# First aggregation pass of a graph network: the mask tile moves to PSUM, and the window sums share four banks

## What is computed

```python
msg = feat[src]
h_sum = jax.ops.segment_sum(msg, dst, num_segments=n)
deg = jax.ops.segment_sum(jnp.ones((src.shape[0],), dtype=feat.dtype), dst, num_segments=n)
h_neigh = jnp.where(deg[:, None] > 0, h_sum / jnp.maximum(deg, 1.0)[:, None], 0.0)
return h_neigh @ W_neigh.T + b_neigh
```

## Time and profile before

| quantity | value |
|---|---|
| median of three runs | 9503.14 us (9498.97 to 9505.79) |
| the profiled execution's own time | 9495.59 us |
| its span in the profile | 9493.7 us |
| first pass, first gather to last add | 33.6 to 1147.5 us |
| busy share over the span: PE, DVE, POOL | 69%, 52%, 73% |

### The profile page before, as it was taken

The page is one execution under the profiler, slowest core; times in us unless marked ns, Lnnn a source line. Parts: engine busy times, 40 slices in busy tenths (PEclk is TensorE's granted clock), DMA queues, the critical chain, the costliest instruction groups (busy, mean ns, idle before and its releaser), DMA issues. The chain is left out here.

```text
span 9493.7 us, 138066 instructions
## 1 busy us (share of the span) xinstructions
PE 6504.4 (69%) x30150; PEld 4954.7 (52%) x30150; DVE 4890.2 (52%) x16263; ACT 1137.3 (12%) x2527; POOL 6905.4 (73%) x7491
## 2 busy tenths in 40 slices
PE   6777656666777788835888866665566668866665
PEld 5656534444666654525777634443455557744443
DVE  7766644333555543685777644444322226744445
ACT  0000000000000003730000000000222227610000
POOL 6777777777777777777777777777677776547775
PEclk6666655555766678558999955555777878965555
DMA  3111112222333332005777621112677765422221
GB/s 86 49 48 50 41 44 53 53 53 53 111 105 105 105 103 74 2 11 153 221 223 222 192 66 53 53 53 58 141 192 193 193 175 149 151 103 53 53 53 53
DMA packets 665600, 935.71 MB, mean 99 GB/s; under 512 B 276165, under 2 KB 444542, under 8 KB 664958
## 3 DMA queue, kind: packets, MB, share of 16 engines
q0 software_dynamic: 271792, 607.35, 24.0%
q1 hardware_dynamic: 294130, 322.66, 10.9%
q10 hardware_dynamic: 99548, 4.42, 0.9%
HBM read 790.86 MB, written 143.03 MB: 98 GB/s over the span
## 5 line engine op out<-in xcount | busy, mean ns | idle before, releaser
L555 PE MATMUL sage_window<-sage_hot,sage_message 128*128 128x128 f32 x4992 | 1443.4, 428 | 683.4 <-DMA sage_message<-t_x,all_src 312.7
L555 PE MATMUL block_window<-block_hot,block_message 128*128 128x128 f32 x3328 | 1184.0, 456 | 714.3 <-DMA block_message<-t_rel,all_src 327.9
L555 PEld LDWEIGHTS sage_window<-sage_hot,sage_message 128*128 128x128 f32 x4992 | 1070.4, 291 | 1056.5 <-issue 719.4
L555 PEld LDWEIGHTS block_window<-block_hot,block_message 128*128 128x128 f32 x3328 | 792.7, 296 | 1081.4 <-issue 623.4
L374 POOL DMA_INDIRECT block_message<-t_rel,all_src x832 | 785.2, 944 | 423.8 <-issue 253.3
L477 DVE TENSOR_TENSOR first_acc<-first_acc,sage_window 128x128 f32 (+1 forms) x1664 | 591.5, 355 | 962.4 <-PE sage_window L555 957.7
L374 POOL DMA_INDIRECT block_message<-in_x,all_src x832 | 849.8, 1021 | 287.8 <-issue 252.9
L1946 POOL DMA_INDIRECT eh_message<-t_q,all_position x880 | 831.3, 945 | 278.2 <-issue 267.4
L374 POOL DMA_INDIRECT gat_message<-t_h,all_src x832 | 791.2, 951 | 262.8 <-issue 252.8
L374 POOL DMA_INDIRECT rgcn_message<-t_rel,all_src x832 | 785.9, 945 | 262.5 <-issue 253.3
L374 POOL DMA_INDIRECT sage_message<-t_x,all_src x832 | 785.7, 944 | 262.2 <-issue 253.2
(11 more groups left out here) (419 smaller groups left out, 10279.0 us busy)
## 6 DMA issues: line engine op xcount, KB each, us to landing
eh_window<-t_p SPq DMA_DIRECT2D x880, 64.0 KB
t_hidden<-eh_hidden SPq DMA_DIRECT2D x110, 512.0 KB, 3.0
sc_rows<-t_hidden SPq DMA_DIRECT2D x110, 512.0 KB, 3.5
eh_low_rows<-t_low SPq DMA_DIRECT2D x110, 256.0 KB
t_rel<-n_h SPq DMA_DIRECT2D x49, 512.0 KB, 2.6
eh_message<-t_q,all_position POOLq DMA_INDIRECT x880
block_message<-in_x,all_src POOLq DMA_INDIRECT x832, 2.5
sage_message<-t_x,all_src POOLq DMA_INDIRECT x832, 2.5
```

The source lines that it names most:

```text
L555: last = nc.tensor.matmul(ps[k][:, b, :], message[u][:, f:f + P], hot[:, u, j * P:(j + 1) * P], start=(j == 0), stop=(j == heads - 1))
```

## The change

In the first pass alone (`places_edges`), the eight windows lie two to a bank in four banks, and `inside` lies in PSUM (two banks' worth, 1024 floats of which 832 are used) where it lay in SBUF. Because two windows share a bank, DVE waits for the second of the two before it adds the first, so that it never reads a bank that PE is writing. In iteration 13 PE waits for `find_starts` before it writes the seventh window of the second half, which shares the bank of `ps_own`; before, it waited ahead of the eighth. The other passes keep their eight windows in eight banks, and their DVE waits are unchanged.

```diff
-        ps = [pb(f"window{k}", [P, outs, P]) for k in range(HU)]
+        if places_edges:
+            banks = [pb(f"windows{k}", [P, 2, outs, P]) for k in range(HU // 2)]
+            ps = [banks[k // 2][:, k % 2] for k in range(HU)]
+            inside = pb("inside", [P, 1024])[:, 0:T]
+        else:
+            ps = [pb(f"window{k}", [P, outs, P])[:] for k in range(HU)]
...
-        inside = sb("inside", [P, T]) if places_edges else None
...
-                    if k == HU - 1:
+                    last_of_bank = u | 1 if places_edges else u
+                    if last_of_bank % HU == HU - 1:
                         dve.wait_ge(e.half_used[h], half0 + it + 1)
                     else:
-                        dve.wait_ge(e.window_ready, done0 + it * (U - 2) + u + 1 - h)
+                        dve.wait_ge(e.window_ready, done0 + it * (U - 2) + last_of_bank + 1 - h)
...
-                    if starts and u == U - 1:
+                    if starts and u == U - 2:
                         pe.wait_ge(starts_used, 1)
```

More of the change, by code:

```diff
@@ L389, in count_block @@
                 dve.wait_ge(counted, j)
-                nc.vector.tensor_scalar(inside[:], m.src_high[:, 0:T], m.iota[:, bass.ds(j, 1)], 0.0, ALU.is_equal, ALU.add,
+                nc.vector.tensor_scalar(inside, m.src_high[:, 0:T], m.iota[:, bass.ds(j, 1)], 0.0, ALU.is_equal, ALU.add,
                                         accum_out=m.in_block[:, bass.ds(j, 1)]).then_inc(counted, 1)
@@ L394, in mask_block @@
                 dve.wait_ge(placed, j + 1)
-                nc.vector.tensor_scalar(inside[:], m.src_high[:, 0:T], m.iota[:, bass.ds(j, 1)], None, ALU.is_equal).then_inc(masked, 1)
+                nc.vector.tensor_scalar(inside, m.src_high[:, 0:T], m.iota[:, bass.ds(j, 1)], None, ALU.is_equal).then_inc(masked, 1)
             def rank_block(j):
                 dve.wait_ge(masked, j + 1)
-                nc.vector.tensor_tensor_scan(rank[:], m.ones[:, 0:1].to_broadcast([P, T]), inside[:], m.block_start[:, bass.ds(j, 1)],
+                nc.vector.tensor_tensor_scan(rank[:], m.ones[:, 0:1].to_broadcast([P, T]), inside, m.block_start[:, bass.ds(j, 1)],
                                              ALU.mult, ALU.add).then_inc(ranked, 1)
@@ L415, in place_block @@
             def place_block():
-                nc.vector.copy_predicated(position[:], inside[:].bitcast(I32), rank[:]).then_inc(placed, 1)
+                nc.vector.copy_predicated(position[:], inside.bitcast(I32), rank[:]).then_inc(placed, 1)
             def own_hots(it):
@@ L427, in own_add @@
                 nodes = m.acc[:, 0:outs, bass.ds(it * P, P)]
-                nc.vector.tensor_tensor(nodes, nodes, ps_own[:], ALU.add).then_inc(own_used, 1)
+                nc.vector.tensor_tensor(nodes, nodes, ps_own, ALU.add).then_inc(own_used, 1)
             def fuse_add(it):
@@ L476, in turn @@
                         dve.wait_ge(own_used, it + 1)
-                    nc.vector.tensor_tensor(window, window, ps[k][:], ALU.add).then_inc(e.window_used, 1)
+                    nc.vector.tensor_tensor(window, window, ps[k], ALU.add).then_inc(e.window_used, 1)
                     if nodes_too and own and u == 2:
```

## The result

The changed kernel takes 9440.4 us, the median of four runs, against 9502.3 us for the kernel before: a ratio of 0.9935, 95% interval 0.9923 to 0.9948, or 61.9 us less. Timed once more, with other kernels beside it, it took 9442.9 us against 9505.0 (0.9936, 0.9921 to 0.9951). The forecast was 9447, with a range of 9438 to 9480.

The account below looks back on a forecast made before the run. POOL's chain of gathers was taken to bound the first pass, PE and DVE following with room left. 63.1 - 6.3 - 0.6 - 0.3 = 55.9 us off the profiled 9495.6 gave a median of 9447 us, range 9438 to 9480.

Parts of the forecast that it names:

- The relief, 63.1 us: Placing stages: running sum and predicated copy no longer hold POOL's gathers, taking 63.1 us off its chain.
- The mask's 0.42 us: DVE's mask, written to PSUM, takes its slow form of 1073 ns, adding 0.42 us per block.
- The sum and the copy at no cost: DVE's running sum and predicated copy, reading the mask from PSUM, take no longer: 0 added.
- The hand-over, 2.43 us: Last add to next half's first add: waiting for two windows raises it from 1.57 to 2.43 us.
- 10.7: Time in us that PE and DVE need for a half that places a block, data always there.
- POOL's wait of 6.3 us: Stage with two blocks per iteration: lateness of DVE beyond what buffers store makes POOL wait 6.3 us.
- 16.3: DVE's lateness in us over the stage with two blocks: 22 halves x 0.74.
- the 10 us that I had for what the buffers store: POOL's buffers let it run ahead, so 10 us of lateness is only stored and made up in later iterations.
- A: Rival: PE and DVE become the bound in both placing stages; 28 us gained, 9475 us; chance 0.19.
- B: Rival: the running sum still holds POOL, gathers stay at 1111 and 1025 ns; 9503 us or slightly more; chance 0.11.
- C: Rival: the running sum takes twice its time reading PSUM; 26 us slower, 9529 us; chance 0.06.
- My point of decision for C, 12.06 us: Length of a placing half from which C decides, 1.35 us above the forecast's 10.7.

Follow-up runs that it names:

- the four kernels: Windows in pairs and mask in SBUF, against the kernel before, with nothing, ranks, ones, or both in PSUM: 9498.7, 9489.5, 9453.9, 9443.5 us.
- pairs_only: The kernel before with only the windows put in pairs, the mask staying in SBUF (the pairs alone): 9498.7 us, ratio 0.9999.
- slow_mask_sbuf: Windows in pairs, ones and ranks in PSUM, mask in SBUF made by the slower form that also sums its output: 9444.2 us, 0.9938 of the kernel before.
- the extra half sum: The changed kernel with a second running sum over half the mask after each block's own: 9470.9 us, 0.9961 of the kernel before.
- the extra sum: The changed kernel with a second running sum over the whole mask after each block's own: 9490.2 us, 0.9986 of the kernel before.

## Why the prediction was right, and where its sum was off

**The relief, 63.1 us: right.** The busy time of the 832 gathers fell by 849.8 - 787.6 = 62.2 us. The last add came 60.3 us earlier: 0.9 us went to idle time ahead of the gathers, and 1.0 to a longer stretch between the last gather and the last add, for which I had 0.6. The reasoning from the adds (one operand in SBUF and one in PSUM, beside gathers of 946 ns) is what the four kernels showed for each operand in turn. The split: against the pairs alone, 45 us from the running sum, 9 from the copy, and, from the traces, some 6 from the mask. In the timelines of the kernel before, the excess of gathers that began inside the three operations was 50, 9 and 1 us (3 for the mask, with those that it held from their middle); the shares of sum and mask depend on how the operations fall against the gathers, which the pairs moved (43, 18 and 6 us in the kernel with the pairs alone). In one thing it was luck: I had counted the mask's slow form only as a cost. With the windows in pairs the fast form held gathers for 6.9 us (`pairs_only`), against 3.2 in the kernel before, and the slow form spared that too.

The rule of the Trainium skill (SBUF — State Buffer, "Who interferes with whom") is borne out in all three clauses: two SBUF inputs hold POOL, one does not, and of the two forms of the mask only the faster one does; the form that also writes its accumulator is the one that the page leaves out of the two-port modes. My prediction left out a condition of the page: for two SBUF inputs it speaks only of a GpSimd instruction that reads SBUF. The gather does, as it takes its row numbers from an SBUF tile.

**The mask's 0.42 us: right** (0.43, from the medians of 648 and 1080 ns). **The sum and the copy at no cost: right**, 1940 and 1071 ns against 1945 and 1078. The Trainium skill's surcharge for PSUM (Perfetto Trace Analysis, "Optimizing Scalar/DVE Operations") did not show where PSUM was read. Where it was written the count's main part grew by 7 ns, 1073 to 1080.

**The hand-over, 2.43 us: the upper end of what came.** In the changed kernel the median in the stage with two blocks was 2.4 us and the mean 2.2, with the shortest 1.6. In 13 of the 22 halves the granted clock was at the lower level all through the hand-over, which took 2.44 us in the mean; in the other 9 it was at the upper level for a part, and they took 1.86. DVE's own work from the first add to the end of the last was 8.0 to 8.8 us, 8.2 in the mean, against the 8.28 of my sum. So a half took 10.38 us (228.3 / 22) and not 10.7. (In that sum I called 409.60 the end of an add. It is the start of the next operation, and the add ends at 409.67; the sum, which goes from start to start, is not touched.)

**POOL's wait of 6.3 us: the term that failed.** It did not wait in a placing stage, in either trace of the changed kernel. 22 halves at 0.38 us over POOL's 10.0 make 8.4 us of lateness, not 16.3, and that fits into the 10 us that I had for what the buffers store. The 10 us are borne out by `slow_mask_sbuf`: its stage with two blocks took 230.8 us, 10.8 over POOL's 220, and near its end POOL began to wait, five times, by 0.2 to 0.5 us each beyond the usual 0.30. The changed kernel's timeline shows the lateness stored and worked off: from the start of a gather to its add it was 6.0 us at the first iteration of that stage, 14.7 us when it ended, and 4.9 us four iterations later. Of the 0.3 us by which a half was shorter than my sum, 0.23 lie in the hand-over above: I took the clock's lower level for every half, from one stretch of 0.50. Without the term the sum is 55.9 + 6.3 = 62.2 us, against 61.9 measured.

**The rivals.** A (28 us gained, PE and DVE the bound in both stages) did not come, but the extra half sum shows its edge: 1.0 us more on DVE per block, and 0.2 more of hand-over, cost 28 us, nearly all of it in the stage with two blocks (255.2 against 228.3 us). B is excluded by the gathers, C by the 1940 ns. My point of decision for C, 12.06 us a half with a block, left out that the halves without one would be shorter: with the extra sum, at 12.5 us a half in the stage with two (274.3 / 22), the kernel was still 15 us faster than before.

## What to carry to other kernels

Where POOL issues indirect DMAs back to back and sets the pace, look at the spread of its instruction's duration, not at its waits: gathers of 1.9 and 2.6 us among ones of 0.94 were DVE's doing, and no wait row told of it. There, a DVE operation with two SBUF inputs is worth giving one input in PSUM, even a constant one. A form of an operation that is faster by itself can hold the gathers where the slower one does not: 7.0 us over the pass for the mask of 0.65 us, nothing for the one of 1.07. A stage whose follower is slightly too slow is free as long as the buffers store its lateness and a later stage works it off, so sum lateness over the stage and compare it with the store before counting it.

## What was not expected

The pairs alone raised PE's clock in the counting stage, in which nothing else had changed. From 60 to 300 us, in the kernel with the pairs alone (busy of PE, PEld, DVE, ACT, POOL, then granted clock):

```profile
60.00:300.00 240.00, 167.14 (x796) 143.04 (x795) 172.84 (x499) 0.00 (x0) 180.16 (x191) 0.73 0.20 52
```

The kernel before has 0.64 there and PE busy for 188 us with as many matmuls; the changed kernel has 0.75. The pairs make PE wait longer at each half: from last add to first add it was 1.5 us in the mean before and 2.2 with the pairs. Why the clock then comes out higher is open; it brought no time, since POOL set the pace.

With the mask in PSUM the read of the accumulator after each count takes 141 ns, against 83 ns with the mask in SBUF, though it writes to the same place in SBUF. Why is not shown.

In the profiled executions the last add of the pass came 60.3 us earlier (1147.1 to 1086.8), but the span is only 51.8 us shorter (9493.7 to 9441.9): later passes took 8.5 us more in that one. The medians of the two kernels differ by 61.9 us, and the executions of one kernel spread over 4 to 14 us, so scatter is enough to explain it. But after the pass the four profiled executions with the mask in PSUM took 8352 to 8357 us, and the six with it in SBUF, the kernel before among them, 8347 to 8351. With one execution of each it is open whether some of this belongs to the change.
